# A decoder layer on one core: shared-expert pieces in halves and gating in fewer steps at the end of attention, and cross-attention scores moved between the two halves of the queries

## What is computed

```python
x = layernorm(x + self_attention(x, qkv_weights))        # 16 heads of 16, causal mask, softmax
q, k, v = xpos(x @ Wq), xpos(ctx @ Wk, inverse), ctx @ Wv  # one head of 256, rotated
x = layernorm(x + (q @ k.T * decay_mask) @ v)
shared = (silu(a) * b) @ sw2                              # a, b = split(x @ sw1 + sb1)
probs = softmax(x @ gate_w + gate_b)                      # 8 experts, each row goes to its best 2
x = layernorm(x + shared + sum over the 2 experts of prob * expert(x))
```

## Time and profile before

| | |
|---|---|
| median of 3 runs | 727.16 us (726.34 to 728.71) |
| the profiled execution | 723.76 us |
| its span | 721.7 us |
| mean granted TensorE clock | 0.990 |
| PE busy, PEld busy | 683.2 us (95%), 588.5 us (82%) |
| DVE, ACT, POOL busy | 489.2, 478.9, 343.1 us |

### The profile page before, as it was taken

How to read it: one execution, slowest core, us unless ns; L and a number is a source line. 1 busy time by engine, 2 the same in 40 slices (tenths; PEclk the granted TensorE clock), 3 DMA queues, 4 the chain that set the end, 5 groups by cost and what they waited for, 6 DMA issues and landing times.

```text
span 721.7 us, 21540 instructions
## 1 busy us (share of the span) xinstructions
PE 683.2 (95%) x6174; PEld 588.5 (82%) x6175; DVE 489.2 (68%) x1563; ACT 478.9 (66%) x1319; POOL 343.1 (48%) x469
## 2 busy tenths in 40 slices
PE   7989999999999999999998899889999999999994
PEld 5868888888888888888887555779999999998653
DVE  3666878888888888888896376445555555554266
ACT  0367888888888888888884242356666666666256
POOL 1001323435645455454455355055665556556495
PEclk9999999999999999999999899999999999999998
DMA  8743367424523233232336024686777777777597
GB/s 306 236 146 114 116 204 240 137 88 147 158 88 96 67 91 105 86 107 83 104 97 198 31 89 143 198 221 126 140 134 139 133 139 136 135 137 130 124 349 261
DMA packets 93947, 104.30 MB, mean 145 GB/s; under 512 B 13200, under 2 KB 86672, under 8 KB 92976
## 3 DMA queue, kind: packets, MB, share of 16 engines
q1 hardware_dynamic: 78480, 79.43, 37.2%
q0 software_dynamic: 14688, 23.26, 16.4%
q10 hardware_dynamic: 704, 0.66, 0.3%
HBM read 62.21 MB, written 41.10 MB: 143 GB/s over the span
## 4 chain that ended last, share of the span: by engine, by line
PE 78%; DVE 5%; DMA 5%; POOL 4%; issue 4%; SPq 3%; ACT 1%; DVEq 0%; POOLq 0%; ACTq 0%
PE ps L1051 15%; PE ps L1060 8%; PE ps L806 6%; PE ps L908 5%; PE ps L794 5%; PE ps L816 4%; PE ps L771 4%; PE ps L739 4%; PE ps L911 4%; PE ps L774 4%; PE ps L932 4%; DMA xg<-sent 3%; POOL first_use L715 2%; PE ps L1038 2%; PE ps L826 2%
## 5 line engine op out<-in xcount | busy, mean ns | idle before, releaser
L1118 ACT ACTIVATE prob<-ps,nmax 128x128 f32<-128x128 f32 x512 | 147.0, 380 | 27.4 <-DVE nmax L1332 27.4
L1051 PEld LDWEIGHTS ps<-xgT,attn_only 128*128 128x128 f32 x1136 | 136.0, 192 | 7.4 <-DVE ghT L1614 2.2
L1051 PE MATMUL ps<-xgT,attn_only 128*128 128x128 f32 x1136 | 138.9, 275 | 1.1 <-ACT xgT L1230 1.1
L674 POOL DMA_INDIRECT total<-rot,result_row x71 | 111.6, 1572 | 36.8 <-issue 34.3
L1332 DVE TENSOR_REDUCE nmax<-ps 128x4 f32<-128x512 f32 x128 | 82.2, 685 | 17.7 <-PE ps L794 17.0
L1614 DVE SCALAR_TENSOR_TENSOR ghT<-ps,attn_only 128x128 f32<-128x128 f32 x142 | 43.3, 347 | 71.0 <-PE ps L1051 59.3
L615 POOL TENSOR_TENSOR rot<-products 128x128 f32<-128x128 f32 x128 | 61.3, 499 | 57.1 <-DVE products L1342 57.0
L1125 ACT COPY pT<-ps 128x512 f32<-128x512 f32 x124 | 74.4, 600 | 20.8 <-PE ps L806 16.4
L806 PE MATMUL ps<-tf,prob 128*128 128x128 f32 x512 | 77.9, 275 | 4.4 <-DVE pT L1447 3.3
L641 POOL DMA_INDIRECT sent<-packets,pos x64 | 63.6, 993 | 35.6 <-PE ps L794 20.9
L1060 PE MATMUL ps<-first_use,ghT 128*128 x284 | 74.9, 386 | 0.0
(11 more groups left out here) (143 smaller groups left out, 1408.1 us busy)
## 6 DMA issues: line engine op xcount, KB each, us to landing
xg<-sent SPq DMA_DIRECT2D x71, 130.5 KB, 2.1
attn_only<-in_L_ffn_rb SPq DMA_DIRECT2D x71, 130.0 KB
first_use<-total SPq DMA_DIRECT2D x12, 512.0 KB, 8.7
total<-zeros POOLq DMA_DIRECT2D x3, 1408.0 KB, 8.0
k_dram<-first_use SPq DMA_DIRECT2D x4, 1024.0 KB, 4.6
attn_only<-in_x_turned SPq DMA_DIRECT2D x32, 128.0 KB, 2.5
attn_only<-k_dram SPq DMA_DIRECT2D x256, 16.0 KB
attn_only<-in_x SPq DMA_DIRECT2D x32, 128.0 KB, 2.7
```

Of the source, the lines that this page charges most:

```text
L674: eng.indirect_dma_start(totals[slot % 2], bass.IndirectOffsetOnAxis(ap=result_row[:, slot:slot + 1], axis=0), yw[:, slot, :], None, compu ...
L1051: mm = eng.matmul(ps[:, 2 * r + half, f * P:(f + 1) * P], w_now[:, r, c, cols:cols + P], xgT[:, r, c, :], start=(c == 0), stop=(c == DC - 1))
L1118: ins = eng.activation(prob[:, t % 2, 4 * u + n, :], SCORE[u][:, n * P:(n + 1) * P], ACT.Exp, bias=nmax[:, t % 2, 4 * u + n:4 * u + n + 1])
```

## The change

- **Scores between the queries' halves.** In every step TensorE makes half `m` = 0 of the cross queries, then the cross scores, then half `m` = 1. VectorE multiplies the scores by the decay ahead of the products of the queries. What each of them waits for stays the same; the queries' semaphore still comes from half 1.
- **Pieces in halves.** The shared expert's pieces are split in halves, and the halves stand at two places of a step (`shared_upper`, where the pieces stood, and `shared_lower`, behind the gate logits). The first piece starts a step earlier, at 32. ScalarE's and VectorE's parts of them move along.
- **Gating in less steps.** For the last three groups the four parts have lags 0, 1, 1 and 2, and the loop ends one step earlier. The scatters of batches 20 to 31 go by the table `LAST_SENT`, two batches in a step, and from step 34 on they stand behind GpSimd's root in the step.
- **`x1` of the last two batches** is turned into bank 4 instead of bank 7.
- **Small moves on VectorE:** the addition of epsilon to the second variance stands ahead of the last mask copy, and the addition of the second quarter's output stands inside the plan instead of ahead of it.

The diff, cut to its core:

```diff
+QUICK = len(GROUPS) - 3
+LAST_SENT = {B: (20, 21), B + 1: (22, 23), B + 2: (24, 25), B + 3: (26, 27), B + 4: (28, 29), B + 6: (30, 31)}
...
 def groups_at(n, lag):
-    return [q for q in range(len(GROUPS)) if group_step(q) + lag == n]
+    return [q for q in range(len(GROUPS)) if group_step(q) + (lag if q < QUICK else (0, 1, 1, 2)[lag]) == n]
...
 def sent_at(n):
-    return [lo + j for q, (lo, size) in enumerate(GROUPS) for j in range(size)
-            if group_step(q) + 4 + (j if size == 4 else 0) == n]
+    if n < B:
+        return [t for t in (n - 12,) if 0 <= t < LAST_SENT[B][0]]
+    return LAST_SENT.get(n, ())
...
+        def turned_x1(t):
+            return ps[:, 7, 0:D] if t < B - 2 else ps[:, 4, 0:D]
...
-        FIRST_STEP, END_STEP = -2, group_step(len(GROUPS) - 1) + 5
+        FIRST_STEP, END_STEP = -2, group_step(len(GROUPS) - 1) + 4
...
@@ GpSimd
+                if n < B + 2:
+                    send(n)
...
                     eng.tensor_tensor(rstd2[:, t % 2, :], mv2[:, t % 2, 1:2], neg_half[:, 0:1], ALU.pow).then_inc(rstd2_set, 1)
+                if n >= B + 2:
+                    send(n)
...
@@ TensorE
-            def shared_between(n):
+            def shared_upper(n):
                 if n == B + 1:
+                    shared_first(0, 1, 2)
+                if n == B + 2:
+                    shared_first(1, 0, 0)
+                if n == B + 3:
+                    shared_first(1, 1, 2)
+                if n == B + 4:
+                    eng.wait_ge(pT_set, 4 * B)
+                    eng.wait_ge(x1T_set, B)
+                    eng.wait_ge(att_set, B)
+                    shared_rows(0, 0, 4)
+                if n == B + 5:
+                    shared_half(2, 0, 1, 0)
+                    shared_first(2, 1, 2)
+                if n == B + 6:
+                    shared_half(2, 1, 1, 2)
+                if n == B + 7:
+                    shared_output(1, 4, 5)
+                    shared_hidden(3, 0, 0)
+
+            def shared_lower(n):
+                if n == B:
                     eng.wait_ge(ffn_in, 16 * (2 + 2 * NE))
                     eng.wait_ge(expd, 4 * B)
                     shared_hidden(0, 0, 0)
+                if n == B + 1:
+                    shared_half(0, 1, 1, 2)
                 if n == B + 2:
-                    shared_hidden(0, 1, 2)
+                    shared_half(1, 0, 1, 0)
                 if n == B + 3:
-                    shared_hidden(1, 0, 0)
+                    shared_half(1, 1, 1, 2)
                 if n == B + 4:
-                    eng.wait_ge(pT_set, 4 * B)
-                    eng.wait_ge(att_set, B)
-                    shared_output(0, 4, 5)
...
+                    shared_first(2, 0, 0)
...
-                    for m in range(2):
-                        for c in range(DC):
-                            mm = eng.matmul(Q_TURNED[:, m, :], xwq_sb[:, c, m * P:(m + 1) * P], x1T[:, t % 2, c, :],
-                                            start=(c == 0), stop=(c == DC - 1))
-                    mm.then_inc(xq_made, 1)
...
-                shared_between(n)
+                    cross_queries(t, 0)
+                if live(n - 4):
+                    cross_scores(n - 4, n)
+                if live(t):
+                    cross_queries(t, 1).then_inc(xq_made, 1)
+                shared_upper(n)
...
@@ VectorE
-                if live(t3):
-                    turned(t3, 2, Q_TURNED, xq_made, pq_set, rot_q_set)
                 if live(t4):
                     eng.wait_ge(scx_made, t4 + 1)
                     eng.tensor_tensor(scx[:, r4, :], SCX, decay, ALU.mult).then_inc(scx_set, 1)
+                if live(t3):
+                    turned(t3, 2, Q_TURNED, xq_made, pq_set, rot_q_set)
...
             planned(eng.tensor_reduce(tile_f[:, 0, :], passed[:, :, :], AX_X, ALU.add))
-            shared_gate(2, 1, 2)
+            add_shared(1, 4, 5)
+            shared_gate(3, 0, 0)
```

More of the change, by code:

```diff
@@ L616, in turn_into, with send @@
                                       ALU.add).then_inc(done, 1)
+            def send(n):
+                for t in sent_at(n):
+                    eng.wait_ge(pos_set, group_of(t) + 1)
+                    eng.wait_ge(scored, 4 * min(n + 1, B))
+                    for j in range(TOPK):
+                        eng.indirect_dma_start(sent, bass.IndirectOffsetOnAxis(ap=pos[:, t, j:j + 1], axis=0),
+                                               packets[:, t % SLOTS, :], None).then_inc(sent_in[t % SLOTS], 16)
             def step(n):
@@ L875, in bank7_read, with cross_queries, cross_scores @@
                     eng.wait_ge(base_set, q + 2)
+            def cross_queries(t, m):
+                for c in range(DC):
+                    mm = eng.matmul(Q_TURNED[:, m, :], xwq_sb[:, c, m * P:(m + 1) * P], x1T[:, t % 2, c, :],
+                                    start=(c == 0), stop=(c == DC - 1))
+                return mm
+            def cross_scores(t, n):
+                eng.wait_ge(rot_k_set, 2 * t + 2)
+                eng.wait_ge(rot_q_set, 2 * t + 2)
+                if live(n - 3):
+                    eng.wait_ge(pk_set, 2 * (n - 3) + 2)
+                else:
+                    bank7_read(n)
+                for m in range(2):
+                    mm = eng.matmul(SCX, rot[:, t % 2, m, :], rot[:, t % 2, 2 + m, :], start=(m == 0), stop=(m == 1))
+                mm.then_inc(scx_made, 1)
             def step(n):
@@ L1011, in step @@
                         eng.wait_ge(kk_set, 4 * NG)
[L1012 removed]
+                    if t < B - 2:
+                        after(eng, gc_set, n - 4)
+                    elif t == B - 2:
+                        eng.wait_ge(pT_set, 4 * B)
+                    else:
+                        eng.wait_ge(x1T_set, t)
                     for c in range(DC):
[L1014 removed]
+                        mm = eng.transpose(turned_x1(t)[:, c * P:(c + 1) * P], x1[:, t % 2, c * P:(c + 1) * P], ident)
                     mm.then_inc(x1_turned, 1)
```

105 lines of the change are left out of this document (45 added, 60 removed).

## The result

| | before | changed |
|---|---|---|
| median | 727.54 us (724.37 to 729.93, 8 runs) | 734.42 us (731.09 to 736.44, 8 runs) |
| the profiled execution, its span | 723.76 us, 721.7 us | 735.22 us, 733.2 us |
| mean granted clock | 0.990 | 0.990 |

The changed kernel is slower: ratio 1.008, 95% interval 1.0051 to 1.0109, which is 5.8 us; between the medians it is 6.9 us. Forecast were 2.0 us more (729.2 us, range 720 to 736). A second measurement (experiment 6) gave 1.0101 (1.0066 to 1.0135), 7.3 us.

The account below looks back on a forecast made before the run. TensorE's order was taken to bound the kernel. Full steps losing 9.0 us and the drain gaining 7.0 us made 2.0 us more on the median of 727.16 us: 729.2 us, range 720 to 736.

Parts of the forecast that it names:

- the forecast's own case: Cross output waits for the queries' products: 7.8 to 10 us lost, 5.5 to 8.5 gained, 726.5 to 731.7 us; chance 0.45.
- `res1` stays long: Full steps: the next projections, waiting for `res2`, decide; 28 by 0.53 us lost, 735.0 us in all; chance 0.15.
- Both rivals with no loss in full steps: Steps have slack, only the drain shows: 720.2 us, chance 0.10; or each step gains 0.39 us: 709.3 us, chance 0.05.
- each step becomes 0.32 us longer: Steps 4 to 31: waits ahead of scores and cross output replace the one at `x2` turned; 28 by 0.32, 9.0 us lost.
- Part 2, the drain: From step 32 to the last prefix sums: filled gaps of TensorE give 7.0 us, between 4 and 10.
- a sign of being wrong: Drain from step 32 to the last prefix: 52 us or more would count against the forecast of some 49.5 us.
- Step 33's scores: Drain: TensorE would still wait 0.77 us ahead of these scores, 1.65 us behind the heads with 0.88 covered.
- Step 34's scores: Drain: 1.15 us wait, since the keys' products wait for ScalarE's copy of the values.
- Step 35's scores: Drain: 1.15 us wait, since they need `base` of the third last group, updated behind `packets` of the same step.
- Step 36: Drain: 0.8 us wait ahead of `x2` turned, since GpSimd's four scatters stand ahead of its root.
- I take the clock as full there: Drain: TensorE would run at full clock, since the stretch ahead of the earlier slow one is now filled.
- Behind the last prefix: A gate ends some 1.6 us behind it, 0.5 us less; the plan ends about 11 us behind, hidden behind padding stores.

Follow-up runs that it names:

- experiment 6: The changed kernel, measured again on another chip: 731.63 us, ratio 1.0101 against the kernel before.
- experiment 1: The kernel before with only the scores' new place and `scx` ahead of the queries' products, old drain: 739.44 us, ratio 1.0145.
- experiment 9: The kernel before with only TensorE's new order, VectorE's order as before: 749.3 us, ratio 1.0323.
- experiment 10: The kernel before with only VectorE's new order, `scx` ahead of the queries' products, TensorE as before: 732.31 us, ratio 1.0095.
- experiment 7: The changed kernel with the loads of the third and fourth quarter of turned `x2` later: 729.91 us, ratio 1.0066.
- experiment 2: The changed kernel with steps 4 to 31 in the old order on both engines, so the drain alone: 721.01 us, ratio 0.991.
- experiment 12: Experiment 8 with step 34's keys' products ahead of step 33's second gating part on VectorE: 710.98 us, ratio 0.9799.
- experiment 5: The kernel before, unchanged, measured again: 723.42 us, ratio 0.9997.
- experiment 3: Experiment 2 with `scx` between the two products of the queries on VectorE: 717.96 us, ratio 0.9847.
- experiment 8: Experiment 3 with the loads of the third and fourth quarter of turned `x2` later: 713.27 us, ratio 0.9849.
- experiment 11: Experiment 3 measured again, loads at their first place: 712.66 us, ratio 0.982.
- experiment 4: The changed kernel with the keys' products ahead of the reciprocal `rden` on VectorE: 733.0 us, ratio 1.0062.

## Why the prediction was right, and where its sizes were off

The sign and the mechanism held; the time came out within the range, 5.2 us above the forecast on the first measurement. That is outside the 726.5 to 731.7 of the forecast's own case, and nearest to the 735.0 of a rival whose mechanism fell. So it is the traces that decide for the forecast's mechanism here, and not the time.

**Part 1, the full steps.** What came as forecast: the scores wait for the keys' products 1.65 us behind the heads, the cross output for the products of the queries, `x2` turned no longer waits, `res1` goes to the short case, and L786 does not wait for `res2`, so the rival "`res1` stays long" fell. Both rivals with no loss in full steps fell with experiment 1. **The step of the sum that was mis-sized is "each step becomes 0.32 us longer".** It measured 11.59 - 11.11 = 0.48 us, so 28 by 0.48 = 13.4 us where the sum had 9.0, inside its bounds of 7.8 to 14.8. The 0.16 us more are twice the 0.08 us that TensorE loses behind each of these two waits: the second half of the queries starts 2.17 us behind the heads where the forecast had 2.09, and L786 5.03 us behind them where it had 4.87 (4.55 before, plus 0.32). The prediction counted each group behind a wait as one in a running row ("starts at 264.79 + 0.44"), although the row it used for the wait had the longer form in it, 0.68 us instead of 0.61. Not every wait costs this much: the two records of L962 took 0.41 us behind their wait and 0.38 without one, 0.03 more. For the scores the number carries over: experiment 9's step was worked out with it, 11.94 us, and measured 11.96.

Neither engine's new order alone helps (experiments 9 and 10). On the whole step only `scx` between the two products takes something off both ends, 0.05 us a step.

**Part 2, the drain.** As a whole the size held where nothing disturbed it: 49.5 us were forecast from step 32's weighing to the last prefix at full clock, and 49.67 us were measured where the clock was full (experiment 7, which has later loads). The first profile, 55.81 us, met what the prediction had named as a sign of being wrong, 52 us or more; a remote stop and the clock are what it has and experiment 7 has not. Experiment 6 took 51.27 us. By itself the drain gave 6.6 us against 7.0 (experiment 2). Its parts were less exact and made up for each other:

- Step 33's scores: 0.77 us forecast. Heads at 411.20 and scores at 412.85 in experiment 6 are 1.65 us with 0.88 of work: 0.77.
- Step 34's scores: 1.15 forecast, 423.00 - 420.62 - 0.44 = 1.94 us measured. The prediction saw ScalarE's copy and overlooked that the change puts two gating parts on VectorE ahead of the keys' products, which took 0.77 us (experiment 12 shows both).
- Step 35's scores: 1.15 forecast, 0.57 us idle in the row. Step 36: 0.8 forecast for GpSimd's scatters, no wait at all in the timeline.
- "I take the clock as full there" was the weak step. In 9 of 14 profiles, of all kernels, step 32's weighing took 1.66 to 1.94 us instead of 1.08, behind the 1.44 us wait of step 31's prefix, which the prediction did not list among the places at risk since it lies ahead of the drain. In single profiles 1.6 us lie between with and without it (experiment 6 against 7), and 3.0 us where two steps had it (experiment 5 against the first profile); it meets old and new drain alike.

The Trainium skill (TensorE: Matmul & The Clock Gate, HAM oscillation) had been cited for waits that put the clock back to half; the rows agree in that 1.2 GHz came behind such a wait in nine profiles, and also show the same 1.44 us of waiting followed by full clock in the five others.

**Behind the last prefix** `tail_rows` came 1.58 us behind it, as forecast (1.6). In the first profile the plan ended 12.2 us behind where 11 were forecast, the padding stores landed at 13.0 instead of 12.8, and the fourth tile started 28.5 us behind the prefix, 27.9 before. But VectorE's remote stop of 2.83 us lay inside this plan. Without one the plan ended 10.9 us behind (experiments 6 and 7), and the fourth tile started 26.4 us behind the prefix in experiment 6, where it was 27.5 for the kernel before on the same chip (experiment 5). So at the fourth tile at least the 0.5 us were gained; from the prefix to the end the two profiles took 282.2 and 281.7 us, so that no gain is left to see there.

**The sum against the runs.** By the steps' length it is 13.4 - 6.6 = 6.8 us, and 5.8 and 7.3 us were measured; by experiment 1's own ratio it is 10.6 - 6.6 = 4.0 us, within the first measurement's interval (3.7 to 7.9 us) and under the second's (4.8 to 9.8 us), though each of the two terms is itself known to 2 us only. The 2.8 us between these two sums stay open. One thing on record bears on them: the executions of the kernel before that ran beside experiment 1 had a mean granted clock of 0.986, those of experiment 1 had 0.991. Span times what the clock lacks to 1 is 10.5 and 6.8 us, by which, as an estimate, 3.7 us of the steps' 13.4 would be hidden. Experiment 2 had 0.991 as well, so the sum of the two ratios may count one gain in clock twice. No profile shows where in the run the kernel before lost them. The forecast added its terms to one profile of before, and stretches of one profile are worth 2 to 3 us either way: the two profiles of before differ by 2.3 us ahead of the first cross output, 3.0 in the drain and 2.1 behind it. Over all 14 profiles the first cross output comes between 74.0 and 78.0 us; the full steps repeat best: 301.6 and 301.7 us before, 314.3 to 314.4 us in the four profiles with the change's order.

## What to carry to other kernels

Where an instruction moves ahead of another, count what its own wait then holds: here scores that had just stopped waiting were put where they wait, and half of the queries stood behind them, so the wait that was to vanish came back longer at the next reader of VectorE's results. Count every wait of TensorE with what follows it, 0.08 us at two places here, when it comes back 28 times. And where two results for the same engine compete for a producer's order, try splitting the longer one; that and the drain's halves without the move of the scores took 1.5 to 2% off (experiments 3, 8, 11 and 12), where the change as a whole lost 0.8%.

## What the runs showed of the hardware

- A group of matmuls that starts behind a wait runs longer. The scores (four records of 128 columns) take 0.68 us instead of 0.61, and the next group starts 0.51 to 0.53 us later instead of mostly 0.46 to 0.48; other groups of four without a wait have 0.44. The cross output (two of 256) takes 0.67 us instead of 0.60, and the next group starts 0.50 to 0.51 us later instead of 0.43 to 0.44. `x2` turned (two of 128) takes 0.41 us instead of 0.38. So it was in nearly all full steps of the kernels here.
- `res1` takes 0.42 us on average when it directly follows the products of the queries (changed kernel, experiments 1, 3, 4 and 10), and 0.70 us when `scx` stands between them (before, experiments 2 and 9), where GpSimd began on the products first. The Trainium skill (SBUF — State Buffer, Who interferes with whom) says that the one issued first wins; the rows agree.
- ScalarE stood still for 3.3 to 4.75 us ahead of one copy in four profiles with the new drain, and for 0.67 us in five others; ScalarE or VectorE also stood still elsewhere in five profiles, four of them on one chip, for 2.1 to 5.1 us, and the trace names nothing that ended these stops. In the profile of after the DMA engines were full at ScalarE's stop, and one instruction transfer of some 16 KB (40 of them are 0.66 MB on the page) lay between 409.0 and 409.5; but experiments 6 and 11 had full DMA engines and one such transfer in the same stretch, and no stop.
